# Attention kernel: value products and row sums two steps behind the scores, across the border of units

## The reference

```python
q  = (x @ Wq).reshape(b, s, 32, 32)            # b = 2, s = 2048, hidden 1024, 32 heads of 32
k, v = split(x @ Wkv)                          # one key and one value head for all 32 query heads
scores = q . k * scale + slope[h] * (kpos - qpos), causal
out = softmax(scores) @ v ;  x = layernorm(x + out @ Wo)
```

## Time and profile before

| | us |
|---|---|
| time before, median of 3 runs (3686.13 to 3690.32) | 3689.47 |
| the profiled execution's own time | 3690.71 |
| its span | 3688.8 |
| granted TensorE clock, mean over the span | 0.983 of full |
| end of the last o_sb copy of attention | about 2784 |
| length of a unit in a row of equal ones, s0 / s1 / s2 / s3 | 20.8 / 33.2 / 47.3 / 60.2 |

### The profile page before, as it was taken

The page is one execution under the profiler, slowest core; times in us unless marked ns, Lnnn a source line. Parts: engine busy times, 40 slices in busy tenths (PEclk is TensorE's granted clock), DMA queues, the critical chain, the costliest instruction groups (busy, mean ns, idle before and its releaser), DMA issues. The chain is left out here.

```text
span 3688.8 us, 56296 instructions
## 1 busy us (share of the span) xinstructions
PE 3509.9 (95%) x20929; PEld 2202.4 (60%) x20929; DVE 2282.9 (62%) x5374; ACT 1867.6 (51%) x3188; POOL 1428.3 (39%) x435
## 2 busy tenths in 40 slices
PE   5999999999999999999999999999995999999998
PEld 4555554555555544555555555545433889898987
DVE  4676676677777753676676667777633444444444
ACT  2556656665676766556666666676673010110100
POOL 1114535544566654124445554575661010101010
PEclk8999999999999999999999999999997999999999
DMA  2211110010000011211100000000004112112121
GB/s 81 53 58 36 52 31 18 24 41 24 24 18 18 18 35 30 69 42 36 53 24 24 24 18 24 18 18 18 13 7 134 52 53 67 63 56 68 51 68 41
DMA packets 157356, 148.09 MB, mean 40 GB/s; under 512 B 8356, under 2 KB 140452, under 8 KB 155016
## 3 DMA queue, kind: packets, MB, share of 16 engines
q1 hardware_dynamic: 157128, 145.07, 13.3%
HBM read 94.13 MB, written 33.62 MB: 35 GB/s over the span
## 5 line engine op out<-in xcount | busy, mean ns | idle before, releaser
L565 ACT ACTIVATE prob<-ps_s,alibi 128x512 f32<-128x512 f32 (+3 forms) x2119 | 1286.6, 632 | 748.1 <-PE ps_s L853 379.7
L506 POOL TENSOR_TENSOR prob<-prob 128x2048 f32<-128x2048 f32 (+1 forms) x240 | 1046.4, 4364 | 975.8 <-ACT prob L565 975.6
L644 DVE TENSOR_REDUCE mxp<-ps_a 128x1 f32<-128x512 f32 x1536 | 978.3, 682 | 298.0 <-PE ps_a L774 286.5
L774 PE MATMUL ps_a<-kmax,qst 97*128 97x512 f32 (+3 forms) x2560 | 956.0, 395 | 36.1 <-DVE mxp L647 17.3
L853 PE MATMUL ps_s<-qst,kexp 97*128 97x512 f32 (+3 forms) x2119 | 863.2, 411 | 43.7 <-ACT prob L565 28.5
L853 PEld LDWEIGHTS ps_s<-qst,kexp 97*128 97x128 f32 x2119 | 399.3, 189 | 565.0 <-ACT prob L565 322.5
L647 DVE CUSTOM_DVE_ANT_0 ps_a<-ps_a,maska 128x128 f32<-128x128 f32 (+3 forms) x1024 | 492.4, 507 | 245.7 <-PE ps_a L774 235.1
L786 PE MATMUL ps_o<-prob,val 128*32 128x512 f32 (+3 forms) x5120 | 603.7, 544 | 8.1 <-ACT prob L565 4.6
L774 PEld LDWEIGHTS ps_a<-kmax,qst 97*128 97x128 f32 x2560 | 486.7, 194 | 111.0 <-DVE mxp L647 31.7
L1056 POOL TENSOR_TENSOR hb_sb<-h_sb,bias_b 128x1024 f32<-128x1024 f32 x32 | 76.7, 2397 | 791.9 <-DVE z_sb L1200 731.3
L786 PE MATMUL ps_sum<-prob,ones 128*32 128x512 f32 (+2 forms) x3072 | 335.0, 508 | 2.4 <-POOL prob L506 2.3
(11 more groups left out here) (154 smaller groups left out, 4106.6 us busy)
## 6 DMA issues: line engine op xcount, KB each, us to landing
wq_raw<-in_L_attn_Wq SPq DMA_DIRECT2D x64, 512.0 KB, 3.9
xs<-in_L_attn_hidden_states SPq DMA_DIRECT2D x8, 2048.0 KB, 8.0
qst<-qst SPq DMA_DIRECT2D x64, 256.0 KB
att_scratch<-at_sb SPq DMA_DIRECT2D x64, 256.0 KB, 2.8
at_raw<-att_scratch SPq DMA_DIRECT2D x32, 512.0 KB, 5.2
x_sb<-in_L_attn_hidden_states SPq DMA_DIRECT2D x32, 512.0 KB, 4.2
out<-z_sb SPq DMA_DIRECT2D x32, 512.0 KB, 3.1
z_sb<-in_L_attn_Wo SPq DMA_DIRECT2D x4, 512.0 KB, 5.4
```

The costliest lines, as they stand in the source:

```text
L506: nc.gpsimd.tensor_tensor(even[:, :, c1:], even[:, :, c1:], odd[:, :, c1:], ALU.add).then_inc(pair_done, 1)
L565: nc.scalar.activation(prob[slot_of(steps + k)][:, h, c0:], ps_s[places[GH * (steps + k) + h][0]][:, c0:], ACT.Exp, bias=alibi_of(g, h, k ...
L644: nc.vector.tensor_reduce(top, ps, AX.X, ALU.max).then_inc(a_done, 1)
L774: last = nc.tensor.matmul(ps[:, 0:cols], qst[buf][0:KR, h, t * P:(t + 1) * P], kmax[0:KR, ring(sg):ring(sg) + cols], start=True, stop=True)
```

## The change

The probabilities' tiles go from eight to six, and two tiles (both0, both1) are new, for the sums of pairs. PV and SM of a step are put two steps later (LAG), SP three steps after the odd step of its pair (PAIR_LAG), both at slot PV_AT of the step then running, **counted over all units**: the last steps' products of a unit come in the first two steps of the next. So does OE, and R starts at slot 6 or 8 of the next unit where it started at slot 0. Where SM and SP had a slot of their own (SM_AT), they now stand directly beside PV. ADDQ and SQ are gone: an s3 unit has 7 SP and 2 SM, and all units together 400 calls. ADD writes into its own tile, waits for the exponentials and for the sum that used that tile last, and where the odd step is on the diagonal it first copies 4 x 128 columns. An exponential waits for PV and for ADD (or SM) of the step six before. The slots at which the other entries are put are new as well.

```diff
-PROBS = 8
+PROBS = 6
+SUMS = 2
+LAG = 2
+PAIR_LAG = 3
...
-CHUNKS_AHEAD = (7, 14, 18, 19)
-A_END = (8, 17, 31, 41)
-A_FROM = (13, 18, 31, 41)
-Q_AT = ((0, 0.5), (0, 1), (1, 1.25), (0, 1.75))
-QE_AT = ((3, 1), (7, 2), (9, 3), (12, 4))
-CT_AT = (12, 22, 35, 42)
-X_AT = ((4, 0.25), (8, 1.75), (19, 1.5), (19, 3.25))
-THIRD = (6, 6, 2, 4)
-QUADS = (0, 0, 0, 1)
-QUAD_AT = 7
-KV_AT = (10, 23, 33, 41)
-VT_AT = (17, 28, 47, 49)
-PV_AT = (1, 1, 2, 1)
-SM_AT = (2, 1, 2, 1)
-WS_AT = (5, 21, 31, 28)
-RECIP_AT = ((0, 2, 3, 4, 11), (0, 2, 3, 5, 14), (0, 2, 5, 7, 18), (0, 2, 4, 5, 20))
+CHUNKS_AHEAD = (8, 14, 15, 19)
+A_END = (10, 17, 33, 41)
+A_FROM = (11, 19, 33, 43)
+Q_AT = ((0, 0.5), (0, 1), (1, 1.5), (0, 1.75))
+QE_AT = ((3, 0), (7, 2), (11, 2), (12, 4))
+CT_AT = (12, 22, 38, 42)
+X_AT = ((4, 0.25), (8, 1.25), (16, 2), (19, 3.25))
+THIRD = (5, 4, 3, 2)
+KV_AT = (10, 25, 33, 43)
+VT_AT = (19, 28, 53, 50)
+PV_AT = (3, 1, 1, 1)
+OE_AT = (3, 1, 1, 2)
+WS_AT = (9, 19, 33, 24)
+RECIP_AT = ((8, 9, 11, 12, 14), (6, 8, 9, 11, 21), (8, 9, 10, 11, 20), (8, 9, 10, 11, 21))
...
+    def over_keys(t):
+
+        gp, kp = STEPS[t - PAIR_LAG] if 0 <= t - PAIR_LAG < len(STEPS) else (0, 0)
+        if kp % 2 and kp // 2 < pairs_summed(gp):
+            out.append(("SP", (gp, kp // 2)))
+        if 0 <= t - LAG < len(STEPS):
+            gp, kp = STEPS[t - LAG]
+            out.append(("PV", (gp, kp)))
+            if kp >= 2 * pairs_summed(gp):
+                out.append(("SM", (gp, kp)))
...
+            if h == PV_AT[s]:
+                over_keys(steps_before(g) + k)
+            if h == OE_AT[s]:
+                take_o(steps_before(g) + k)
         if k % 2 and k // 2 < summed:
             out.append(("ADD", k // 2))
-        if k % 4 == 3 and k // 4 < quads:
-            out.append(("ADDQ", k // 4))
...
+        both = [sb(ctx, f"both{i}", [P, GH, QB], F32) for i in range(SUMS)]
...
-                        pool.wait_ge(pv_done, START + steps + k + 1)
-                        nc.gpsimd.tensor_tensor(even[:, :, c1:], even[:, :, c1:], odd[:, :, c1:],
+                        if pair >= SUMS:
+                            pool.wait_ge(sm_done, START + sums_until_pair(pair - SUMS))
+                        if c1:
+                            nc.gpsimd.tensor_copy(dst[:, :, 0:c1], even[:, :, 0:c1])
+                        nc.gpsimd.tensor_tensor(dst[:, :, c1:], even[:, :, c1:], odd[:, :, c1:],
                                                 ALU.add).then_inc(pair_done, 1)
...
+            def slot_free(t):
+
+                if t >= 0:
+                    gp, kp = STEPS[t]
+                    act.wait_ge(pv_done, START + t + 1)
+                    if kp < 2 * pairs_summed(gp):
+                        act.wait_ge(pair_done, START + pairs_before(gp) + kp // 2 + 1)
+                    else:
+                        act.wait_ge(sm_done, START + sums_until(gp, kp))
...
                         if h == 0:
-                            act.wait_ge(sm_done, START + max(0, steps + k + 1 - PROBS))
+                            slot_free(steps + k - PROBS)
```

More of the change, by code:

```diff
@@ L72, in pairs_summed, with pairs_before, sums_before, sums_until @@
     return ktiles(g) // 2 - 1 if full_tiles(g) else 0
[L75 to L94, removed]
+def pairs_before(g):
+    return sum(pairs_summed(x) for x in range(g))
+def sums_before(g):
+    return sum(ktiles(x) - pairs_summed(x) for x in range(g))
+def sums_until(g, k):
+    return sums_before(g) + min(k // 2, pairs_summed(g)) + max(0, k - 2 * pairs_summed(g)) + 1
+def sums_until_pair(p):
+    g = max(x for x in range(UNITS) if pairs_before(x) <= p and pairs_summed(x))
+    return sums_until(g, 2 * (p - pairs_before(g)))
 def ring(sg):
@@ L210, in plan_unit, with take_o @@
     recip_at = {x: part for part, x in enumerate(RECIP_AT[s])}
-    summed, quads = pairs_summed(g), quads_summed(g)
+    summed = pairs_summed(g)
+    def over_keys(t):
[7 more added lines that the diff above has]
+                out.append(("SM", (gp, kp)))
+    def take_o(t):
+        if 0 <= t - LAG and STEPS[t - LAG][1] == ktiles(STEPS[t - LAG][0]) - 1:
+            out.append(("OE", STEPS[t - LAG][0]))
     for k in range(n):
@@ L219, in plan_unit @@
             out += [x for x in at.get(i, []) if x[0] != "X"]
[L220 to L227, removed]
+            if h == PV_AT[s]:
+                over_keys(steps_before(g) + k)
+            if h == OE_AT[s]:
+                take_o(steps_before(g) + k)
         if k % 2 and k // 2 < summed:
             out.append(("ADD", k // 2))
-        if k % 4 == 3 and k // 4 < quads:
-            out.append(("ADDQ", k // 4))
[L232 to L235, removed]
+    if g == UNITS - 1:
+        for t in range(len(STEPS), len(STEPS) + PAIR_LAG):
+            over_keys(t)
+        take_o(len(STEPS) + LAG - 1)
     return out
+STEPS = [(g, k) for g in range(UNITS) for k in range(ktiles(g))]
 def program(nc, x, wq, wkv, wo, w, bias, la, lb, gate_w, gate_b, out):
@@ L500, in step @@
                     if what == "ADD":
-                        k = 2 * arg
+                        k, pair = 2 * arg, pairs_before(g) + arg
                         c1 = max(0, k + 1 - full_tiles(g)) * P
                         even, odd = (prob[slot_of(steps + k + i)] for i in range(2))
+                        dst = both[pair % SUMS]
                         pool.wait_ge(e_done, START + GH * (steps + k + 2))
-                        pool.wait_ge(pv_done, START + steps + k + 1)
-                        nc.gpsimd.tensor_tensor(even[:, :, c1:], even[:, :, c1:], odd[:, :, c1:],
+                        if pair >= SUMS:
[3 more added lines that the diff above has]
+                        nc.gpsimd.tensor_tensor(dst[:, :, c1:], even[:, :, c1:], odd[:, :, c1:],
                                                 ALU.add).then_inc(pair_done, 1)
[L508 to L511, removed]
             units(prologue, step, lambda count: divide(UNITS - 1))
@@ L567, in step @@
                     if what == "OE":
-                        act.wait_ge(pv_done, START + steps + ktiles(g))
-                        act.wait_ge(at_done, START + g)
+                        act.wait_ge(pv_done, START + steps_before(arg + 1))
+                        act.wait_ge(at_done, START + arg)
                         nc.scalar.activation(o_sb[:], ps_o[:], ACT.Copy).then_inc(o_copied, 1)
@@ L667, in invert @@
                 if part == 0:
-                    dve.wait_ge(sm_done, START + steps_before(g + 1))
+                    dve.wait_ge(sm_done, START + sums_before(g + 1))
                     nc.vector.transpose(sum_t[:].rearrange("p b d -> p (b d)"), ps_sum[:]).then_inc(sum_turned, 1)
@@ L781, in turn_max, with over_keys @@
                 nc.tensor.transpose(ps_a[bank_of(count)][0:GH * QT, 0:P], mx[:], ident[:]).then_inc(a_full, 1)
-            def over_keys(g, ps, weights, k):
+            def over_keys(g, ps, weights, k, src):
                 c0 = max(0, k - full_tiles(g)) * P
                 for h in range(GH):
-                    last = nc.tensor.matmul(ps[h * DH:(h + 1) * DH, c0:], weights,
-                                            prob[slot_of(steps_before(g) + k)][:, h, c0:],
+                    last = nc.tensor.matmul(ps[h * DH:(h + 1) * DH, c0:], weights, src[:, h, c0:],
                                             start=k == 0, stop=k == ktiles(g) - 1)
@@ L858, in step @@
                     if what == "PV":
[L859 to L864, removed]
+                        gp, kp = arg
+                        at = steps_before(gp) + kp
+                        pe.wait_ge(e_done, START + GH * (at + 1))
+                        if kp == 0:
+                            pe.wait_ge(o_copied, START + gp)
+                        over_keys(gp, ps_o, val[:, key_tile(gp, kp)], kp, prob[slot_of(at)]).then_inc(pv_done, 1)
+                    if what in ("SM", "SP") and arg[1] == 0:
+                        pe.wait_ge(sum_turned, START + arg[0])
                     if what == "SM":
-                        pe.wait_ge(e_done, START + GH * (steps + arg + 1))
-                        over_keys(g, ps_sum, ones[:], arg).then_inc(sm_done, 1)
+                        gp, kp = arg
+                        at = steps_before(gp) + kp
+                        pe.wait_ge(e_done, START + GH * (at + 1))
+                        over_keys(gp, ps_sum, ones[:], kp, prob[slot_of(at)]).then_inc(sm_done, 1)
                     if what == "SP":
[L869 to L873, removed]
+                        gp, pair = arg[0], pairs_before(arg[0]) + arg[1]
+                        pe.wait_ge(pair_done, START + pair + 1)
+                        over_keys(gp, ps_sum, ones[:], 2 * arg[1], both[pair % SUMS]).then_inc(sm_done, 1)
             units(prologue, step, lambda count: None)
```

## The result

The changed kernel takes **3717.98 us** (median of 4 runs, 3710.8 to 3725.4) against 3688.98 before in the same comparison: 1.008 times as long, 95% interval 1.0056 to 1.0103. I had forecast slower, at 3699, between 3666 and 3714; the loss is 29 us where I gave 10, and the time lies outside that range. The profiled execution, 3710.8 us with a span of 3709.0, is the shortest of the four; the mean granted clock was 0.970 to 0.974 in the four (before: 0.983 in the profiled one).

What follows compares the result with a forecast made beforehand. TensorE was taken to set the pace. Terms +15 - 5 - 4 - 1 - 2 + 1 + 1 + 5 = +10 us on the profiled 3690.7 gave 3701, the median 1.2 lower: 3699 us, range 3666 to 3714.

Steps and rivals of the forecast that it cites:

- DVE, the step that is moved: R's parts 0 to 2 (1.7 us) move to later slots; in s0 +1 us over 16 units (-5 to +6).
- My chain: s0: DVE's work through reduction, turning product and shift's DMA to the next unit's first S; unit 21.0 us, not 20.8.
- Late PV in s0: End of s0 units: 0.7 us a unit of PE's time comes free, up to 11 us over 16 units.
- Rival A: s0, slots 4 to 12: PE's freed time is kept, -14 us instead of +1; whole 3672 or 3665; chance 0.36.
- Second round of sums: s3: one SQ replaced by two SP, 16 calls more, +14 to +16 us of PE work, 5 absorbed.
- s3's last units: Units 30, 31, 62, 63: about 18 late PV of 0.25 us saved, -4 us (0 to -8).
- s2, 0 (-8 to +8): s2: QE entries packed closer, chunks spread over two slots more; no row prices this, 0 between -8 and +8 us.
- s1, R in the QE stretch: s1: R's 1.7 us fall between slots 6 and 9, where DVE and ACT are full; +5 us (0 to +12).
- POOL, hidden: POOL: 48 copies of 512 columns, 0 to 1.3 us each, hidden because the SP needing them comes 10 slots later.
- s3 units 60.8 to 61.1: Sign that the forecast is right: steady s3 units lengthen from 60.2 us to 60.8 to 61.1.
- PV's switch of 0.1: Everywhere: switching into PV costs about 0.10 us, so PV would still start 0.1 behind its neighbour.

Runs made afterwards that it cites:

- e15: Changed kernel with each score product of s0 units repeated twice more at slots 4 to 10 (14 useless products a unit): 3698.9 us, 1.0026 of before.
- e9: Kernel before, with parts 1 and 2 of R in s0 units (0.96 us of DVE work) moved to slots 8 and 9, no lag: 3688.9 us.
- e10: Changed kernel, with DVE's two turns of the row sums in s0 units cut from 512 to 32 columns from the second unit on: 3715.6 us.
- e3: Kernel before, with only the second round of sums given up (QUADS all 0; 16 sum calls more, 16 POOL adds fewer): 3701.3 us, 1.0033 of before.
- e4: Kernel before, with the changed kernel's slots in s2 units alone and no lag: 3674.6 us.
- e6: Changed kernel with the lag of two kept, but s0's chunks, QE, third bank and WS at the slots of before: 3745.5 us.
- e1: Changed kernel, with the four QE entries of s0 units spread over slots 3 to 6, not all at slot 3: 3727.7 us, 1.0101 of before.
- e5: Changed kernel with a lag of one step, its chunks kept; in s0 QE at slots 3 to 6, PV at 1, row sums turned at 2 to 4: 3752.0 us.
- e7: Changed kernel with a lag of one step and s0's slots as before the change, row sums turned at slots 2 to 4: 3716.6 us, 1.0083 of before.
- e2: Kernel before, with all four QE entries of s0 units packed at slot 3: 3782.3 us.

## Why the prediction was wrong in size

The sign was right by luck. All that lies outside s0 adds up to -15.3 us (20.3 less 35.6): with s0 units as long as before, or at the 20.5 us of unit 32, the change would have made the kernel faster. By the prediction's own steps, profiled execution against profiled execution:

- **DVE, the step that is moved; s0 at +1 us, ends -5 and +6: this is the step that failed.** Measured: +35.6. My chain took every instruction at the clock of before and let PE's freed microseconds be worth nothing. They cost: the change took 2 us of wide products out of slots 5 and 6, where the Q products are over and PE lives on what ACT and DVE let through, and TensorE's clock halved for 6.8 us of a steady unit. e15 shows the cause, and unit 32 fits it. The chain's own mechanism, R on DVE, is worth nothing in s0 at these slots (e9, e10). The length it gave, 21.0 us, is 0.5 over what unit 32 takes at full clock, so it wasn't right for that case either. No rival had the clock in it.
- **Late PV in s0, up to 11 us of PE's time free:** freed as said, and without other work in its place this was the harm. Rival A asked whether DVE would let PE use the time; where the clock held (unit 32) most of it wasn't used either, 20.5 us for A's 20.1 or less.
- **Second round of sums, +14 to +16, 5 absorbed:** e3 gives +12 by medians, 13 between the profiled executions, and 1.0 us a unit by lengths, none absorbed.
- **s3's last units, -4 (0 to -8):** in the range. Units 30, 31, 62 and 63 together went from 218.7 to 215.7 us, -3.0, and against e3, which has the added calls as well, -2.6. All of s3 came to +6.6, where my terms gave +15 - 5 - 4 = +6.
- **s2, 0 (-8 to +8):** -20.7. "No row prices this" was true, but I then took zero and ends that were too narrow; e4 shows it as a matter of slots. This miss hid more than half of the one in s0.
- **s1, R in the QE stretch, +5 (0 to +12):** +3.2 over both segments, 0.2 us a steady unit. The last unit of its second segment alone rose by 4.3 us, with the clock at 0.50 for 10 us of it; before, that fall came in the first segment only. e9 and e10 touched s0 alone, so whether it is R isn't shown.
- **POOL, hidden:** right. The copy takes 0.61 us (0 to 1.3 given), and no exponential waited for POOL. The Trainium skill ("GPSIMD Engine Reference", Engine selection) has one-input operations at about line rate and two-input ones about twice as slow as on DVE. The estimate from it was 0.65, half of the two-input price, and the trace agrees: 0.61 for the copy, 1.28 for the two-input product of that size. View of the new tiles:

```profile
L523 POOL TENSOR_TENSOR both<-prob x240: 3445/4578/4609, 288.1 to 2800.9; 128x2048 f32<-128x2048 f32 x96, 128x1536 f32<-128x1536 f32 x24
L522 POOL COPY both<-prob x48: 609/611/628, 306.3 to 2800.3; 128x512 f32<-128x512 f32 x48
```

- **s3 units 60.8 to 61.1, the sign of a right forecast:** 60.8 to 60.9. PV's switch of 0.1 stayed: in an s3 unit PV starts 0.32 us after the chunk before it. The loader waited for exponentials before PV 254 times up to 2780 us (386 before), and the waits that went brought little: s3 gave back 0.4 us a unit.

How much of s0's +35.6 us is the clock's? It stood at 0.50 for 82 us more there, and a microsecond at half clock costs at most half a microsecond: 41 us at most. e15, with the falls mostly gone and its filler still in, is 21.3 us over before in s0, and by medians 19 us under the changed kernel. Its steady units take 21.6 us for unit 32's 20.5, so by an estimate from these two most of what is left, 1.1 us a unit, is the filler. Of the 35.6 us, 12 lie in the last three units of the two s0 segments, among them the one that prepares the next segment.

## What to carry to other kernels

Taking waits away from a saturated engine by moving its work elsewhere is two edits, and the place that loses the work has to be priced too: here TensorE's clock halved behind three microseconds of 14, 51 and 74%, for longer than the stretch itself. Look for the thinnest microseconds of a stage first, and think twice before moving the widest products out of them. Test a suspicion of this kind by adding useless products: a unit that gets shorter by more work is hard to read in another way. Where a change bundles a new order with new slots, try the slots alone: here the gain in s2 came from them (e4), and the loss in s0 stayed with the lag of two when the slots went back (e6). And when a change moves the event by which you mark the end of a stage, mark it by another.

## What the runs showed of the hardware

- Three microseconds with PE busy for 14, 51 and 74% brought the granted clock from 1.00 to 0.50 with no single stop over 1 us (changed kernel); one of 37% between full ones didn't (before), nor one of 26% (changed kernel, unit 32), nor 83 and 60% (e15). In e1 the fall came two full microseconds behind one of 29%. After the fall PE was busy without a break at 0.50 for 6.8 us before the clock rose (changed kernel); in lag-one kernels the falls lasted 3.4 us (e5, e7), and behind a stop of 3 us one lasted 23.9 us, with PE busy for 22.5 us of it (e2).
- At a granted clock of 0.50 a call of eight 512-column products took 1.7 us from start to start, against 0.88 at 1.00.
- A copy of 128x512 on POOL took 0.61 us, a two-input operation of that size (the product that divides the output) 1.28 (before).
